# A macaron block on one core: z split straight out of PSUM, y evicted by halves, all jobs in a new order

## The chip, the core and the metric

The kernel runs on one core of a Trainium2 chip. Its time is the device time in microseconds (us) of one execution. TensorE (PE in the profile) multiplies, VectorE (DVE), ScalarE (ACT) and GpSimd (POOL) compute on tiles, SyncE (SP) starts most transfers. SBUF is the core's memory for operands, PSUM the one that TensorE writes to. Each engine works through its own queue of instructions in the order in which the program emits them, and waits on semaphores for the others.

## The reference

Four batches of 1024 tokens of width 128 in float32 go through three residual steps:

```python
x = L0_attn_x                                   # (4, 1024, 128)
x = x + 0.5 * ffn(layernorm(x))
x = x + mixer(layernorm(x))                     # x of this line is layernormed first; the mixer adds its own input too
x = x + 0.5 * ffn(layernorm(x))

def ffn(h):                                     # one routing decision for each batch of 1024 tokens
    logits = mean over the tokens of h @ gate_w # 8 experts
    top 2, their softmax weights normalised to sum 1
    out = sum of weight_e * (gelu(h @ w1[e] + b1[e]) @ w2[e] + b2[e])    # F = 512

def mixer(h):
    xn = clip(norm_scale * h / rms(h)); xc = silu(causal conv of 4 taps of xn)
    dt, v, gate = split(xc @ in_proj_w); dt = clip(softplus(dt + dt_bias))
    v = rope(v) * dt
    a decaying sum of v along the tokens, by chunks of 32, with a carry from chunk to chunk
    out = (heads mixed by a 16x16 matrix) * sigmoid(gate) @ out_proj_w;  return h + out
```

## The kernel before

The tokens of a batch lie in xt, [128 tokens, 8 tiles, 128 features], and stay in SBUF for the whole kernel. The two feed-forward steps are eight passes: pass q is batch q % 4, passes 0 to 3 are the first step and 4 to 7 the second. The mixer of batch b runs between pass b and pass b + 4, spread over the passes in between, so that its work on VectorE, ScalarE and GpSimd lies beside TensorE's feed-forward work.

**A pass.** VectorE takes the statistics of x (pass_stats), GpSimd makes 1/sqrt(var + eps) of them (pass_rstd: f_ve, then f_rstd), VectorE normalises into f_tok (pass_normalise), TensorE transposes that into aux_ps (pre_norm). ScalarE's turn_z copies aux_ps back into f_tok and sums over the tokens on the way (L570, into zsum, with an accumulator read), then rounds that copy to z_hi (L574), the part of z that the fast float32r matmul takes whole. VectorE's split_z subtracts z_hi from the copy in f_tok, which gives the rest z_lo (L1125). TensorE's pre_route (L953) multiplies zsum by the gate matrix, again into aux_ps; VectorE's route takes the two best experts of it (MAX, FIND_INDEX), and their weights are loaded and split into high and low parts likewise. The tile of the split first weights is w1_parts in the order of the instructions and w_parts in the trace.

**A slot.** Each pass has 8 slots (2 experts x 4 tiles of F), 64 in all. up(slot) is 6 matmuls of 128x512 into hid_ps: w_hi by z_hi, w_hi by z_lo, w_lo by z_hi, each for two halves of the tokens (L845). gelu(slot) on ScalarE makes hid of it (L639). down(slot) adds the slot's part to y in y_ps: in passes 0 to 4 with 8 matmuls for 8 token tiles (L873, in float32, y with tokens on the partitions); in passes 5 to 7 y is computed transposed, most slots by parts hid_hi and hid_lo in float32r (6 matmuls of 128x512, L898), the others whole. hid_ps has 2 buffers, hid 4, y_ps one. down is emitted a good slot after its up. The last three slots are computed apart (down_tail).

**The end of a pass.** In passes 0 to 4, update_x adds y_ps times coef to xt by halves (L1248), and waits for bias_added as well: token_bias on GpSimd computes the weighted b2 of the two experts (L486, L489) and adds it to xt with an accumulating DMA from GpSimd's queue (L494). The first down of the next pass waits until update_x has read y_ps, half by half. In passes 5 to 7 pass_out on ScalarE evicts y to yt with scale and bias (L670), in one piece in passes 5 and 6 and in two in pass 7; post on TensorE transposes yt into aux_ps (L965), and update_x adds that to xt. There the first down of the next pass waits for all of yt, once.

**aux_ps.** It is one PSUM tile of 128x1024, and all of TensorE's work beside up and down goes through it: norm, route, post, and the mixer's norm, dt, v, gate, heads and out. take_aux links them in the order in which they are emitted: whoever writes next waits until the last reader of the previous content is done, by halves where that reader works by halves. Before the change the reader of a norm is L570 (semaphore zt_ready).

**The order.** It is written out by hand, as numbers. A slot is 40 ticks; up(s) stands at tick 40 s on TensorE, gelu(s) at 40 (s + 1) on ScalarE, down(s) at 40 s + 98, or + 132 by parts. The table AT gives for each engine the tick of every other job. Each engine's program runs over the ticks and emits what stands at each; ticks are no times, they set an engine's order alone. Semaphores do the rest, so a job that is emitted early holds its whole engine until its input is there.

## Time and profile before

| | us |
|---|---|
| median of 3 runs | 260.31 (260.23 to 260.34) |
| profiled execution | 260.13 |
| its span in the trace | 258.3 |
| outside the span | 1.8 |
| TensorE busy in the span | 251.7 |

The span runs from the first to the last instruction of the profile. Sums against the trace are made against the 260.13 of the same execution, whose mean granted clock of TensorE was 0.997 of full. In the profile, busy time of a matmul is modelled at its end, and matmuls overlap a little, so an operation's row in a timeline may start a tenth or two before its piece in the chain of waits. A time in brackets behind a row is how long the engine sat idle before it, and for whom. A chain piece is a stretch of the sequence of work that ended last; where nothing waits, consecutive pieces touch.

### The profile page before, as it was taken

To read this page: it belongs to the slowest core of one execution; us is meant where nothing else is said; L and a number is where in the kernel's file an instruction comes from. 1 tells how busy PE (TensorE), PEld (TensorE's weight loads), DVE (VectorE), ACT (ScalarE), POOL (GpSimd) and SP (SyncE) were. 2 spreads that over 40 slices of the span, in tenths; PEclk is the share of its full clock that TensorE was granted. 3 is DMA by queue.
4 is the path that set the end of the run, shared out by engine and by line. 5 is a ranking of instruction groups with operands and counts; after the bars stand their busy time and mean duration, and the time that the engine had idled before them with its cause. 6 is when DMAs were issued, how large, how long until landed. Compare 5 with 4: busy or idle time off the path is not lost.

```text
span 258.3 us, 4609 instructions
## 1 busy us (share of the span) xinstructions
PE 251.7 (97%) x1540; PEld 218.6 (85%) x1540; DVE 211.1 (82%) x536; ACT 195.1 (76%) x236; POOL 82.9 (32%) x90
## 2 busy tenths in 40 slices
PE   7999999999999999999999999999999999999994
PEld 7979999998998979899979999878678687887894
DVE  4656587798589799999999999999999998675712
ACT  1255664866999877968848989999989957979650
POOL 5225306920019700995502957500306002000000
PEclk9999999999999999999999999999999999999998
DMA  6589749855100077430700700700007000570022
GB/s 194 176 255 338 121 81 362 177 221 206 63 0 0 13 94 242 47 38 9 260 0 0 81 4 0 247 0 0 0 4 246 0 0 3 155 229 24 0 84 82
DMA packets 21975, 26.18 MB, mean 101 GB/s; under 512 B 1280, under 2 KB 17152, under 8 KB 21952
## 3 DMA queue, kind: packets, MB, share of 16 engines
q1 hardware_dynamic: 15312, 22.39, 26.6%
q0 software_dynamic: 5280, 2.88, 9.3%
q10 hardware_dynamic: 1360, 0.62, 0.9%
q8 instruction: 12, 0.20, 0.3%
q14 instruction: 11, 0.09, 0.1%
HBM read 16.98 MB, written 6.29 MB: 90 GB/s over the span
## 4 chain that ended last, share of the span: by engine, by line
PE 91%; ACT 3%; issue 2%; DMA 1%; DVE 1%; POOL 0%; SPq 0%; DVEq 0%; ACTq 0%; POOLq 0%
PE hid_ps L845 32%; PE y_ps L873 28%; PE y_ps L898 10%; PE aux_ps L984 5%; PE aux_ps L940 4%; PE aux_ps L1016 3%; PE aux_ps L1005 3%; PE hid_ps L1023 2%; PE y_ps L917 1%; PE aux_ps L965 1%; ACT hid L639 1%; DMA m_tok<-wpack_dram 1%; ACT late L729 1%; PE y_ps L1028 1%; PE hid_ps L917 1%
## 5 line engine op out<-in xcount | busy, mean ns | idle before, releaser
L845 PE MATMUL hid_ps<-z_hi,w_parts 128*128 128x512 f32 x256 | 83.9, 410 | 0.4 <-ACT w_parts L592 0.4
L873 PEld LDWEIGHTS y_ps<-w_sb,hid 128*128 128x128 f32 x640 | 77.1, 192 | 4.3 <-DMA w_sb<-wpack_dram 0.8
L873 PE MATMUL y_ps<-w_sb,hid 128*128 128x128 f32 x640 | 78.1, 275 | 0.4 <-ACT hid L639 0.4
L639 ACT ACTIVATE hid<-hid_ps,w_sb 128x1024 f32<-128x1024 f32 x56 | 61.8, 1109 | 16.7 <-PE hid_ps L845 16.4
L845 PEld LDWEIGHTS hid_ps<-z_hi,w_parts 128*128 128x128 f32 x256 | 45.2, 189 | 9.5 <-issue 1.4
L845 PE MATMUL hid_ps<-z_lo,w_parts 128*128 128x512 f32 x128 | 40.1, 394 | 0.0
L1223 DVE TENSOR_TENSOR hid_lo<-hid,hid_hi 128x1024 fp32r<-128x1024 f32 x19 | 22.9, 1218 | 7.8 <-ACT hid_hi L646 7.8
L845 PEld LDWEIGHTS hid_ps<-z_lo,w_parts 128*128 128x128 f32 x128 | 24.0, 188 | 5.6
L646 ACT ACTIVATE hid_hi<-hid 128x1024 fp32r<-128x1024 f32 x19 | 19.6, 1054 | 1.3 <-PE y_ps L898 1.2
L486 POOL TENSOR_SCALAR bias_tok<-w_sb,coef 128x128 f32<-128x128 f32 x10 | 7.3, 734 | 39.1 <-DMA w_sb<-wpack_dram 25.2
L1110 DVE TENSOR_SCALAR f_tok<-xt,f_mv,f_rstd 128x128 f32<-128x128 f32 x64 | 17.7, 351 | 2.0 <-POOL f_rstd L464 1.9
L1089 DVE BATCH_NORM_STATS2 f_stat<-xt 128x6 f32<-128x128 f32 x64 | 13.1, 276 | 5.4 <-DMA xt<-x_dram 5.3
L530 POOL TENSOR_SCALAR small<-mix_tmp 128x32 f32<-128x32 f32 x4 | 4.3, 1080 | 40.7 <-DVE cumd L1337 40.7
L1294 DVE SCALAR_TENSOR_TENSOR xc<-xs,vec_sb,xc 128x1024 f32<-128x1024 f32 x12 | 15.3, 1276 | 1.8 <-ACT xc L692 1.7
L474 POOL TENSOR_SCALAR f_ve<-f_mv 128x8 f32<-128x8 f32 x7 | 2.4, 343 | 44.4 <-DVE f_mv L1092 44.3
L464 POOL TENSOR_TENSOR f_rstd<-f_ve,neg_half 128x8 f32<-128x8 f32 (+1 forms) x9 | 14.5, 1608 | 2.9 <-DVE f_ve L1096 2.3
L639 ACT ACTIVATE hid<-hid_ps,b_first 128x1024 f32<-128x1024 f32 x8 | 8.9, 1110 | 7.0 <-PE hid_ps L845 6.9
L684 ACT ACTIVATE xt<-xt,m_shift,m_gain 128x128 f32<-128x128 f32 x32 | 12.7, 483 | 0.0
L898 PE MATMUL y_ps<-hid_hi,w_hi 128*128 128x512 f32 x38 | 12.5, 410 | 0.0
L898 PE MATMUL y_ps<-hid_lo,w_hi 128*128 128x512 f32 x38 | 11.9, 394 | 0.0
L898 PE MATMUL y_ps<-hid_hi,w_lo 128*128 128x512 f32 x38 | 11.8, 393 | 0.0
L1125 DVE TENSOR_TENSOR z_lo<-f_tok,z_hi 128x1024 fp32r<-128x1024 f32 x7 | 8.6, 1233 | 3.3 <-ACT z_hi L574 3.1
(149 smaller groups left out, 465.4 us busy)
## 6 DMA issues: line engine op xcount, KB each, us to landing
w_parts<-w_split SPq DMA_DIRECT2D x12, 512.0 KB, 4.1
w_split<-mix_tmp SPq DMA_DIRECT2D x8, 512.0 KB, 4.9
w_sb<-wpack_dram SPq DMA_DIRECT2D x9, 322.5 KB, 4.0
xt<-bias_tok POOLq DMA_DIRECT2D x5, 512.0 KB, 6.5
late<-wpack_dram SPq DMA_DIRECT2D x2, 1024.0 KB, 7.1
w_sb<-wpack_dram SPq DMA_DIRECT2D x6, 258.5 KB, 4.3
xt<-x_dram SPq DMA_DIRECT2D x3, 512.0 KB, 8.4
out_dram<-xt SPq DMA_DIRECT2D x3, 512.0 KB, 3.2
```

The source lines that it names most:

```text
L464: nc.gpsimd.tensor_tensor(f_rstd[:, tiles], f_ve[:, tiles], neg_half[:, 0, tiles], ALU.pow).then_inc(done, 1)
L639: nc.scalar.activation(hid[:, slot % HBUF, :], hid_ps[:, slot % 2, :], ACT.Gelu, bias=bias).then_inc(hid_ready, 1)
L646: nc.scalar.activation(hid_hi[:, slot % 2, :], hid[:, slot % HBUF, :], ACT.Copy).then_inc(hid_hi_ready, 1)
L684: nc.scalar.activation(xt[:, b, t, :], xt[:, b, t, :], ACT.Identity, bias=m_shift[:, t:t + 1], scale=m_gain[:, t:t + 1]).then_inc(x_plus_h, 1)
L845: last = nc.tensor.matmul(hid_ps[:, slot % 2, cols], w, z[:, q % 2, cols], start=first, stop=end)
L873: last = nc.tensor.matmul(y_ps[:, cols], hid[:, slot % HBUF, cols], w_sb[:, q % 2, k, W2_AT + f * P:W2_AT + (f + 1) * P], start=t == 0 and ...
L898: last = nc.tensor.matmul(y_ps[:, cols], wt, src[:, cols], start=t == 0 and i == 0, stop=slot + 1 in (SLOTS * (q + 1), TAIL[0]) and end)
L984: last = nc.tensor.matmul(aux_ps[:, cols], wt[:, w, :], z[:, cols], start=first, stop=end)
L1089: V.bn_stats(f_stat[:, t, :], xt[:, b, t, :]).then_inc(f_stats_step, 1)
L1110: V.tensor_scalar(f_tok[:, t, :], xt[:, q % B, t, :], f_mv[:, t, 0:1], f_rstd[:, t:t + 1], ALU.subtract, ALU.mult).then_inc(f_norm_done, 1)
L1223: V.tensor_tensor(hid_lo[:, slot % 2, :], hid[:, slot % HBUF, :], hid_hi[:, slot % 2, :].bitcast(F32), ALU.subtract).then_inc(hid_lo_ready, 1)
L1294: V.scalar_tensor_tensor(xc[:, :], xs[:, k:k + N], conv_w[:, k:k + 1], xc[:, :], ALU.mult, ALU.add).then_inc(conv_step, 1)
```

## The change

Three things are changed.

**z.** turn_z is one ScalarE instruction in place of two: it rounds aux_ps to z_hi and sums on the way. split_z subtracts z_hi from aux_ps. f_tok is no longer written by ScalarE. So the last reader of a norm's aux_ps is z_lo (zlo_ready), for which the next writer of aux_ps, mostly route, waits; pass_normalise no longer waits for z_lo.

**y of passes 5 to 7.** pass_out always evicts two halves. In the last slot of such a pass, down runs all terms of the first half of the tokens and then those of the second, and a new semaphore y_half_up tells ScalarE of the first. The next pass's first down waits for yt by halves, and post too.

**The order.** Every number of AT is set anew; the slots' own offsets stay.

```diff
-        "f_norm": {1: 189, 2: 389, 3: 809, 4: 1149, 5: 1509, 6: 1829, 7: 2166},
+        "f_norm": {1: 189, 2: 309, 3: 789, 4: 1169, 5: 1509, 6: 1806, 7: 2166},
...
-        "f_bias": {0: 144, 1: 375, 2: 877, 3: 974, 4: 1363},
+        "f_bias": {0: 289, 1: 513, 2: 718, 3: 1205, 4: 1432},
...
                 act.wait_ge(f_turned, q + 1)
                 act.wait_ge(logits_up, q)
-                f_feat = f_tok[:, :, :].rearrange("p t d -> p (t d)")
-                nc.scalar.activation(f_feat, aux_ps[:, :], ACT.Copy, accum_out=zsum[:, 0:1]).then_inc(zt_ready, 1)
-                act.wait_ge(zt_ready, q)
                 if q >= 2:
                     act.wait_ge(hid_up, SLOTS * (q - 1))
-                nc.scalar.activation(z_hi[:, q % 2, :], f_feat, ACT.Copy).then_inc(zhi_ready, 1)
+                nc.scalar.activation(z_hi[:, q % 2, :], aux_ps[:, :], ACT.Copy,
+                                     accum_out=zsum[:, 0:1]).then_inc(zhi_ready, 1)
...
-                for i, cols in enumerate(parts_of(q, N)):
-                    act.wait_ge(hid_used, (SLOTS * (q + 1) if q < PASSES - 1 else TAIL[0]) + i)
+                for half in range(2):
+                    cols = slice(half * HALF, (half + 1) * HALF)
+                    if half:
+                        act.wait_ge(hid_used, last_turned(q) + 1)
+                    else:
+                        act.wait_ge(y_half_up, turned_passes(q + 1))
                     nc.scalar.activation(yt[:, cols], y_ps[:, cols], ACT.Identity,
                                          bias=bias2[:, q % 2, :], scale=coef[:, q % 2, 0:1]).then_inc(yt_ready, 1)
...
-                if t == 0 and q and not in_tokens(q - 1):
-                    pe.wait_ge(yt_ready, turned_passes(q))
...
+                steps = [(i, half) for i in range(len(terms)) for half in range(2)]
+                if slot == last_turned(q):
+                    steps = [(i, half) for half in range(2) for i in range(len(terms))]
...
+                    elif t == 0 and i == 0 and q:
+                        pe.wait_ge(yt_ready, 2 * turned_passes(q) - 1 + half)
...
+                    if slot == last_turned(q) and end and half == 0:
+                        last.then_inc(y_half_up, 1)
...
             def pre_norm(q):
-                free = take_aux(zt_ready, q, q)
+                free = take_aux(zlo_ready, q + 2, q + 2)
...
-                pe.wait_ge(zt_ready, q)
+                pe.wait_ge(zhi_ready, q + 1)
                 free = take_aux(index_ready, q + 1, q + 1)
...
                     dve.wait_ge(f_turned, q)
-                    if q >= 2:
-                        dve.wait_ge(zlo_ready, q + 1)
...
-                V.tensor_tensor(z_lo[:, q % 2, :], f_tok[:, :, :].rearrange("p t d -> p (t d)"),
+                V.tensor_tensor(z_lo[:, q % 2, :], aux_ps[:, :],
                                 z_hi[:, q % 2, :].bitcast(F32), ALU.subtract).then_inc(zlo_ready, 1)
```

Three places show how the new numbers move the instructions. For the same operation the line number of after is a few higher than that of before.

**First, GpSimd in pass 0.** f_ve and f_rstd are the statistics of pass 1 and of pass 2; bias_tok and the DMA are token_bias of pass 0. Before:

```order
L474 TENSOR_SCALAR f_ve<-f_mv 128x8
L464 TENSOR_TENSOR f_rstd<-f_ve,neg_half 128x8
L486 TENSOR_SCALAR bias_tok<-w_sb,coef 128x128 x2
L489 TENSOR_TENSOR bias_tok<-bias_tok 128x128
L494 DMA xt<-bias_tok 128x8x128
L474 TENSOR_SCALAR f_ve<-f_mv 128x8
L464 TENSOR_TENSOR f_rstd<-f_ve,neg_half 128x8
```

After:

```order
L475 TENSOR_SCALAR f_ve<-f_mv 128x8
L465 TENSOR_TENSOR f_rstd<-f_ve,neg_half 128x8
L475 TENSOR_SCALAR f_ve<-f_mv 128x8
L465 TENSOR_TENSOR f_rstd<-f_ve,neg_half 128x8
L487 TENSOR_SCALAR bias_tok<-w_sb,coef 128x128 x2
L490 TENSOR_TENSOR bias_tok<-bias_tok 128x128
L495 DMA xt<-bias_tok 128x8x128
```

The bias and its DMA have moved behind the statistics of pass 2. Those wait for VectorE's BN_AGGR of pass 2, on VectorE at the same place. Here f_tok is the normalise of pass 1 (L1110, L1112) and z_lo the rest of pass 1's z; before:

```order
L1110 TENSOR_SCALAR f_tok<-xt,f_mv,f_rstd 128x128 x8
L1089 BN_STATS f_stat<-xt 128x6 x8
L1092 BN_AGGR f_mv<-f_stat 128x2 x8
L1217 TENSOR_SCALAR w_sb<-w_sb,ratio 128x512
L1125 TENSOR_TENSOR z_lo<-f_tok,z_hi 128x1024
L1418 TENSOR_SCALAR proj_sb<-proj_sb 128x512
```

After:

```order
L1112 TENSOR_SCALAR f_tok<-xt,f_mv,f_rstd 128x128 x8
L1148 ISA
L1148 TENSOR_TENSOR w1_parts<-late,w1_parts 128x256
L1152 TENSOR_TENSOR w1_parts<-m_tok,w1_parts 128x256
L1127 TENSOR_TENSOR z_lo<-aux_ps,z_hi 128x1024
L1219 TENSOR_SCALAR w_sb<-w_sb,ratio 128x512
L1093 BN_STATS f_stat<-xt 128x6 x8
L1096 BN_AGGR f_mv<-f_stat 128x2 x8
L1174 MAX top_v<-aux_ps 128x8
```

z_lo and the scaling of the second weights (w_sb) stood behind the statistics of pass 2 and now stand ahead of them.

**Second, TensorE at slot 42.** aux_ps<-proj_sb,late is m_out of batch 2, the six matmuls from silu are m_dt of batch 3, and hid_ps is an up. Before:

```order
L845 MATMUL hid_ps<-z_hi,w1_parts 128x512 x2
L1016 MATMUL aux_ps<-proj_sb,late 128x128 x8
L845 MATMUL hid_ps<-z_hi,w1_parts 128x512 x2
L845 MATMUL hid_ps<-z_lo,w1_parts 128x512 x2
L845 MATMUL hid_ps<-z_hi,w1_parts 128x512 x2
L984 MATMUL aux_ps<-silu_hi,proj_hi 128x512
L984 MATMUL aux_ps<-silu_hi,proj_lo 128x512
L984 MATMUL aux_ps<-silu_lo,proj_hi 128x512
L984 MATMUL aux_ps<-silu_hi,proj_hi 128x512
```

After:

```order
L848 MATMUL hid_ps<-z_hi,w1_parts 128x512 x2
L1020 MATMUL aux_ps<-proj_sb,late 128x128 x8
L988 MATMUL aux_ps<-silu_hi,proj_hi 128x512
L988 MATMUL aux_ps<-silu_hi,proj_lo 128x512
L988 MATMUL aux_ps<-silu_lo,proj_hi 128x512
L988 MATMUL aux_ps<-silu_hi,proj_hi 128x512
L988 MATMUL aux_ps<-silu_hi,proj_lo 128x512
L988 MATMUL aux_ps<-silu_lo,proj_hi 128x512
L848 MATMUL hid_ps<-z_hi,w1_parts 128x512 x2
```

The up that stood between m_out and m_dt has moved behind m_dt.

**Third, TensorE at the end of pass 6.** aux_ps<-gate_sb,zsum is route 7, aux_ps<-ident,yt is post 5, y_ps a down by parts. Before:

```order
L898 MATMUL y_ps<-hid_hi,w2_lo 128x512 x2
L898 MATMUL y_ps<-hid_lo,w2_hi 128x512 x2
L953 MATMUL aux_ps<-gate_sb,zsum 128x8
L845 MATMUL hid_ps<-z_hi,w1_parts 128x512 x2
L845 MATMUL hid_ps<-z_lo,w1_parts 128x512 x2
L845 MATMUL hid_ps<-z_hi,w1_parts 128x512 x2
L965 MATMUL aux_ps<-ident,yt 128x128 x8
```

After:

```order
L906 MATMUL y_ps<-hid_hi,w2_lo 128x512 x2
L906 MATMUL y_ps<-hid_lo,w2_hi 128x512 x2
L848 MATMUL hid_ps<-z_hi,w1_parts 128x512 x2
L848 MATMUL hid_ps<-z_lo,w1_parts 128x512 x2
L848 MATMUL hid_ps<-z_hi,w1_parts 128x512 x2
L959 MATMUL aux_ps<-gate_sb,zsum 128x8
L969 MATMUL aux_ps<-ident,yt 128x128 x8
```

The up that stood between route 7 and post 5 now stands ahead of both.

## Rows read from the trace of the kernel before

**Rows 1.** The profile's page, busy time of each engine, share of the span, instructions.

```profile
PE 251.7 (97%) x1540; PEld 218.6 (85%) x1540; DVE 211.1 (82%) x536; ACT 195.1 (76%) x236; POOL 82.9 (32%) x90
```

**Rows 2.** Windows: busy us of PE, PEld, DVE, ACT, POOL; PE clock, DMA share, GB/s.

```profile
180.00:200.00 20.00, 19.45 (x86) 14.69 (x85) 19.41 (x41) 18.84 (x21) 6.82 (x5) 1.00 0.23 81
...
240.00:258.00 18.00, 14.77 (x93) 12.93 (x92) 6.43 (x10) 6.98 (x7) 0.00 (x0) 0.97 0.21 60
```

**Rows 3.** Timelines of TensorE and ScalarE, first down; then the chain: start, us, what.

```profile
14.29 0.42 ACT L609 ACTIVATE w_parts<-m_tok 128x256 fp32r<-128x256 f32 x1 [1.00 <-DMA m_tok<-wpack_dram]
...
15.85 2.02 PE L873 MATMUL y_ps<-w_sb,hid 128*128 128x128 f32 x16 [0.39 <-ACT hid L639]
...
24.22 0.87 PE aux_ps L940 x8
...
43.42 1.78 PE y_ps L873 x16
```

**Rows 4.** Chain, one TensorE timeline row at 186.99, and the waits for L570.

```profile
83.05 2.04 PE y_ps L873 x16
...
219.83 0.26 PE aux_ps L953 x2
...
233.58 1.61 PE y_ps L898 x6
...
236.57 1.39 PE y_ps L898 x6
...
186.99 1.96 PE L898 MATMUL y_ps<-hid,w_sb 128*128 128x512 f32 x4 [0.55 <-ACT hid L639]
...
PEld aux_ps L953 <- ACT f_tok L570: 0.6, 2, 0.3
```

**Rows 5.** By line: duration ns min/median/max, first and last start; last, one timeline row.

```profile
L574 ACT ACTIVATE z_hi<-f_tok x7: 1057/1058/1060, 28.7 to 219.6; 128x1024 fp32r<-128x1024 f32 x7
...
L1125 DVE TENSOR_TENSOR z_lo<-f_tok,z_hi x7: 1217/1226/1270, 29.8 to 224.9; 128x1024 fp32r<-128x1024 f32 x7
...
L670 ACT ACTIVATE yt<-y_ps,bias,coef x4: 772/991/1208, 204.9 to 247.7; 128x1024 f32<-128x1024 f32 x2, 128x512 f32<-128x512 f32 x2
...
150.33 1.22 DVE L1362 TENSOR_TENSOR late<-aux_ps,rope_sb 128x1024 f32<-128x1024 f32 x1
```

**Rows 6.** Timeline of GpSimd (POOL), 16 to 32 us.

```profile
19.51 1.20 POOL L486 TENSOR_SCALAR bias_tok<-w_sb,coef 128x128 f32<-128x128 f32 x2
...
21.57 1.67 POOL L494 DMA_DIRECT2D xt<-bias_tok  x1 [0.31 <-POOL bias_tok L489]
...
26.37 0.36 POOL L474 TENSOR_SCALAR f_ve<-f_mv 128x8 f32<-128x8 f32 x1 [3.14 <-DVE f_mv L1092]
...
26.82 1.67 POOL L464 TENSOR_TENSOR f_rstd<-f_ve,neg_half 128x8 f32<-128x8 f32 x1
```

**Rows 7.** Timeline of VectorE (DVE), 20 to 44 us.

```profile
24.08 1.65 DVE L1089 BATCH_NORM_STATS2 f_stat<-xt 128x6 f32<-128x128 f32 x8 [1.97 <-DMA xt<-x_dram]
...
40.37 1.65 DVE L1248 SCALAR_TENSOR_TENSOR xt<-y_ps,coef,xt 128x512 f32<-128x512 f32 x2 [1.39 <-PE y_ps L873]
```

**Rows 8.** Landing of the bias DMA (L494), and SP's DMA issues in its timeline.

```profile
DMA to landing us min/median/max: 6.4/6.5/9.5
...
34.50 1.49 SPq L412 DMA_DIRECT2D w_sb<-wpack_dram  x2
...
36.10 20.16 SPq L420 DMA_DIRECT2D w_split<-mix_tmp  x8
```

**Rows 9.** Timeline of GpSimd, the carry of batch 2.

```profile
157.98 2.24 POOL L531 TENSOR_SCALAR ncd<-cumd 128x32 f32<-128x32 f32 x1
```

**Rows 10.** Timeline of VectorE ahead of the mixer's add of batch 2.

```profile
172.03 1.28 DVE L1403 SCALAR_TENSOR_TENSOR late<-late,aux_ps 128x512 f32<-128x512 f32 x2
...
173.23 1.22 DVE L1307 TENSOR_TENSOR silu_lo<-silu,silu_hi 128x1024 fp32r<-128x1024 f32 x1
```

**Rows 11.** Timeline of VectorE, route of pass 7.

```profile
220.41 0.16 DVE L1179 FIND_INDEX8 top_i<-top_v,aux_ps 128x8 uint32<-128x8 f32 x1
```

More of the change, by code:

```diff
@@ L90 @@
[L90 to L95 removed]
+        "c_split_rest": {0: 113, 1: 168},
@@ new lines @@
+        "m_cos": {0: 767, 1: 1131, 2: 1476, 3: 1800},
+        "m_decay": {0: 779, 1: 1080, 2: 1437, 3: 1817},
+        "m_u": {0: 814, 1: 1210, 2: 1514, 3: 1912},
+        "m_carry": {0: 829, 1: 1193, 2: 1563, 3: 1910},
+        "m_dstep": {0: 830, 1: 1170, 2: 1533, 3: 1925},
+        "m_u2": {0: 860, 1: 1225, 2: 1565, 3: 1948},
+        "m_scan": {0: 893, 1: 1237, 2: 1609, 3: 1970},
+        "m_scan2": {0: 914, 1: 1263, 2: 1639, 3: 1995},
+        "m_gated": {0: 982, 1: 1356, 2: 1683, 3: 2062},
@@ L117 @@
+        "y_out": {5: 1992, 6: 2310, 7: 2500},
     },
     "pool": {
[L119 to L123 removed]
+        "f_rstd": {1: 40, 2: 170, 3: 543, 4: 887, 5: 1451, 6: 1648, 7: 1949},
+        "f_bias": {0: 289, 1: 513, 2: 718, 3: 1205, 4: 1432},
@@ L129 @@
+        "y_store": {4: 2259, 5: 2447, 6: 2477},
     },
@@ L889, in down @@
                     terms = [(w2, hid[:, slot % HBUF, :], None)]
-                for i, (wt, src, ready) in enumerate(terms):
-                    if ready:
-                        pe.wait_ge(ready, split_slots(slot))
-                    for half in range(2):
-                        cols = slice(half * HALF, (half + 1) * HALF)
-                        end = i == len(terms) - 1
-                        if t == 0 and i == 0 and q and in_tokens(q - 1):
-                            pe.wait_ge(x_updated, 2 * q - 1 + half)
-                        last = nc.tensor.matmul(y_ps[:, cols], wt, src[:, cols], start=t == 0 and i == 0,
-                                                stop=slot + 1 in (SLOTS * (q + 1), TAIL[0]) and end)
-                        if slot == TAIL[0] - 1 and end and half == 0:
-                            last.then_inc(hid_used, 1)
+                steps = [(i, half) for i in range(len(terms)) for half in range(2)]
+                if slot == last_turned(q):
+                    steps = [(i, half) for half in range(2) for i in range(len(terms))]
+                for i, half in steps:
+                    wt, src, ready = terms[i]
+                    if ready and half == 0:
+                        pe.wait_ge(ready, split_slots(slot))
+                    cols = slice(half * HALF, (half + 1) * HALF)
+                    end = i == len(terms) - 1
+                    if t == 0 and i == 0 and q and in_tokens(q - 1):
+                        pe.wait_ge(x_updated, 2 * q - 1 + half)
+                    elif t == 0 and i == 0 and q:
+                        pe.wait_ge(yt_ready, 2 * turned_passes(q) - 1 + half)
+                    last = nc.tensor.matmul(y_ps[:, cols], wt, src[:, cols], start=t == 0 and i == 0,
+                                            stop=slot == last_turned(q) and end)
+                    if slot == last_turned(q) and end and half == 0:
+                        last.then_inc(y_half_up, 1)
                 last.then_inc(hid_used, 1)
             def down_tail():
-                pe.wait_ge(yt_ready, turned_passes(PASSES) + 1)
+                pe.wait_ge(yt_ready, 2 * turned_passes(PASSES))
                 pe.wait_ge(w2_scaled, scaled_passes(PASSES))
```

132 lines of the change are left out of this document (60 added, 72 removed), and 6 rows, old and new, of the table AT.

## The prediction

> **What bounds the kernel now.** Read the busy times first: TensorE works 251.7 us of the span of 258.3, VectorE 211.1, ScalarE 195.1 [rows 1]. Then the table by stretches, for where TensorE's 6.6 idle us lie: 0.55 in 180 to 200 and 3.23 after 240 [rows 2]; most of the other 2.8 lies before the first down. The ends are code that the change leaves alone: the warm-up, the first routing and the load that the first up waits for, and the last VectorE updates and stores. So what the change can win is what TensorE waits or works slowly between its first down and its last post. There the profile has four kinds of places, all small; I look at each with TensorE's timeline, where a down that has waited for ScalarE shows either idle time in brackets or a duration above its fellows':
> - the first down, idle 0.39 before it and 2.02 long where a down that hasn't waited takes 1.78 [rows 3]: 0.63. Ahead of gelu 0 on ScalarE stands L609, which waited 1.00 for its load [rows 3].
> - down 19, 2.04 instead of 1.78 [rows 3, 4]: 0.26, gelu 19 behind a table load.
> - down 43, 0.55 idle, and I give 0.2 to the slow restart: 0.75 [rows 4].
> - the routing matmuls of passes 6 and 7, whose weight load waits 0.3 each time for L570, of which about 0.14 reaches the matmuls: 0.28; and down 56, 1.61 instead of 1.39, behind the eviction of y: 0.22 [rows 4].
>
> Together 2.14 us. That is the ceiling of a gain: 260.13 - 2.1 = 258.0. In the stretch with the long wait VectorE is busy 19.41 of 20 us and ScalarE 18.84 [rows 2], so a freed engine helps only where the other one isn't late as well.
>
> **The z part.** It removes L574 seven times, 7 x 1.06 = 7.4 us of ScalarE [rows 5]; the accumulator read stays. It lies beside TensorE and is worth what the waits above are worth, no more. z_lo stays one VectorE instruction, now with PSUM as one source. L1125 from SBUF takes 1.23, and L1362, also a tensor_tensor of 128x1024 but out of PSUM, 1.22 [rows 5]: cost nothing. What does change is that aux_ps is held until z_lo has read it: route now waits for z_lo, one VectorE instruction later than before, and the next pass's normalise waits no longer. Where route stands behind an up or a down (all passes), 1.2 us fit in that cover; without it route would cost TensorE up to 1.2 each.
>
> **The y part.** Passes 5 and 6 evict in two pieces of 0.77 us where one piece takes up to 1.21 [rows 5]: up to 0.33 more of ScalarE twice, but the first half can start while TensorE still does the other. I take down 56's 0.22 back, and nothing else.
>
> **The order: the places that the old cover has left.** All terms are on TensorE, against "due", the old start less the 0.63 of the first down.
>
> *The bias of pass 0.* This is the large one. GpSimd (POOL) made bias_tok at 19.51 and started its DMA at 21.57; only then it took the statistics of pass 2, f_ve and f_rstd, 26.37 to 28.49 [rows 6]. Now both come first. f_rstd 2 needs VectorE's f_stats 2, and that now stands behind z_lo 1 and the scaling of w2. norm 1 leaves TensorE at 24.22 + 0.87 - 0.63 = 24.5 [rows 3] (its place is unchanged), z_hi 1 is one instruction with its accumulator read, 1.15 to 1.2: 25.7; z_lo 1.23: 26.9; the scaling of 512 columns, 0.4 by estimate: 27.3; from the start of the statistics to that of f_ve as before (24.08 to 26.37 [rows 6, 7], 2.3): 29.6; f_ve and f_rstd 2.1: 31.7; bias from 19.51 to 21.57, 2.1: the DMA starts at 33.8 instead of 21.57. It takes 6.4 to 9.5 us to land [rows 8]: 6.4 or 6.5 mostly, 9.5 the first time, beside large loads. In the old trace SP's queue issues w_sb twice at 34.50 and w_split from 36.10 on [rows 8], and this comes at about the same time now, so the bias won't be alone: I take 9.5 as the low end of "shared", 43.3, and as the high end an even split, where 6.4 less 1.67 for issuing [rows 6] counts twice: 33.8 + 1.67 + 9.46 = 44.9. The Trainium skill ("DMA: Bandwidth & Descriptors", Queues, rings and completion order) says that a DMA engine takes turns between its queues packet by packet, which speaks for the even split; by a free road it would land at 40.2.
> Who waits: update 0 (L1248), 1.65 for two halves [rows 7], waits for the DMA; down 8 writes y_ps and waits for the first half, 0.8 and a hop after the landing: 0.9. Down 8 started at 43.42 and is due at 42.8 [rows 3]. So a landing by 41.9 costs nothing, 43.3 costs 1.4, 44.9 costs 3.0. I take 43.8 (nearer to the row than to the split, since not all loads are there at once): **1.9**. Behind update 0 on VectorE stand the splits for SP, m_stats 0 and z_lo 2, which have slack of a slot or two.
>
> *Five small ones.*
> - gelu 38: m_carry 2 now starts on GpSimd about 158.75. In the old trace one of its steps, on 32 columns, took 2.24 us [rows 9]. With a chain of 3.0 us in all I get ScalarE's decay and its table loads out so that down 38 is 0.3 late; each us more is one more, so a step like the old one would make it about 1.3. I take 0.3.
> - m_out 2 and m_dt 3 now stand directly behind each other on TensorE, with no up between. m_dt 3 writes aux_ps and must wait for m_add's first half, which follows gated and silu_lo on VectorE. These ran from 172.03 to 174.4 [rows 10]; a half of the add is one more piece like a half of gated, 0.64, so 175.1. m_out ends at 174.5: 0.6. Bounds 0 (if m_add gets in ahead) and 1.3.
> - down 40 needs w2_lo, now behind f_stats 6: 0.15.
> - gelu 47 now stands behind m_decay 3 and its table loads: 0.4, set between down 19's 0.26 and down 43's 0.55, which waited for ScalarE in the same way; 0 to 1.3.
> - post 5 now stands directly behind route 7, which it follows in aux_ps; it waits until MAX and FIND_INDEX have read the logits, 219.83 to 220.57 in the old trace [rows 4, 11]: 0.6 with the hop.
>
> Sum 2.05. That eats the 2.14 won.
>
> **The sum.** 260.13 - 2.14 + 2.05 + 1.9 = 261.9. The profiled execution lies 0.18 under the median (260.31), so the median of after is **262.1**.
>
> **Rivals.**
> *A, the bias lands late, as above.* Landing 43.3 to 44.9, small ones 1.5 to 2.3: 261.1 to 263.4 in the median.
> *B, the bias is in time.* For: a lone one took 6.4, and 33.8 + 6.4 = 40.2 is before 41.9. Against: the loads at 34.50. Small ones as reckoned: 260.31 - 0.1 = 260.2, no change.
> *C, not slower, and faster: the bias is in time and the small waits stay out.* Mechanism: 7.4 us less on ScalarE let gelu run ahead, so that carry, silu_lo and the table loads are reached earlier than I reckon from old times; it decides from about 1 us of lead on either engine at 160 to 180. 260.31 - 2.14 + 0.3 = 258.5. For: VectorE's 19.41 of 20 shows that it, not data, paces that stretch, and it loses the wait behind L574. Against: VectorE itself has not a microsecond less to do.
> *D, the bias late and the small waits out:* 258.5 + 1.9 = 260.4, no change.
> *E, more slips.* Everything behind update 0 arrives late and a carry of 4.0 us costs 1.3: 263.0 to 264.
> *F, the change doesn't do what it says* (z_hi and its sum in one instruction takes as long as two, as would show in a ScalarE row of 2 us at z_hi): then there is no lead, and the 2.14 are not won: 263 to 264; I count it with E.
>
> **How the numbers follow.** A 0.48, B 0.14, C 0.17, D 0.13, E with F 0.08. The prediction is A's, 262.1. The range leaves out C and E's upper part: 259.8 to 263.2. A measurement of this kernel can tell about 0.2%, 0.52 us, from no change. Faster than 259.8: C and a bit of B and D, 0.20. Within: most of B and D, 0.21. Slower than 260.8: A, E and a bit of D, 0.59.
>
> **What would show it.** In TensorE's waits a new one of 1 to 3 us at the down line, at about 43, for VectorE's update, which itself waits for the DMA xt<-bias_tok; if there is none, A's main step is wrong. A wait at post at about 221 for top_i, and one at the projection at about 174.5 for xt. No ScalarE wait for m_tok ahead of gelu 0, down 19 at 1.78, and no idle time at 187. The forecast is wrong if the bias's DMA starts clearly before 33 us, or if the sum of the small waits is under 1 us.

## The result

The changed kernel takes 262.07 us in the median of 6 runs (261.72 to 264.76), the kernel before, measured beside it, 260.22 (259.27 to 260.34). The ratio is 1.009, with a 95% interval of 1.0051 to 1.0128: slower by about 1%. Measured once more beside the kernel before, it took 262.77 against 259.51, ratio 1.0109 (1.0088 to 1.0129). The ratios of this document leave out two executions, of 317 and 424 us, whose granted clock was low.

The page of after, the row that answers to [rows 1]: TensorE has 254.3 us of work in a span of 263.0, ScalarE 188.6 instead of 195.1.

```profile
PE 254.3 (97%) x1540; PEld 220.4 (84%) x1540; DVE 211.8 (81%) x536; ACT 188.6 (72%) x231; POOL 76.1 (29%) x90
```

This profiled execution took 264.76 us, 2.7 more than the median of its kernel, so I take the figures below from a second profiled execution of the same kernel (label after_again, 262.88 us, span 261.1) wherever the two differ, and come back to the 2.7 at the end. TensorE's waits in that second one (engine, what it waited to do, for whom: us in total, times, longest):

```profile
PE y_ps L876 <- ACT hid L638: 1.8, 1, 1.8
...
PE aux_ps L988 <- ACT mix_tmp L718: 0.6, 1, 0.6
...
PE aux_ps L969 <- DVE top_i L1181: 0.5, 1, 0.5
...
PE aux_ps L988 <- DVE xt L1414: 0.3, 1, 0.3
```

The first is at down 8, at 44 us. Who was late there, in the timelines of the first profile of after: GpSimd's DMA of the bias and its landing, SP's load of w_sb, then VectorE's update 0, ScalarE's gelu 8 and TensorE's down 8. They answer to [rows 3, 6 to 8].

```profile
29.80 0.24 POOL L475 TENSOR_SCALAR f_ve<-f_mv 128x8 f32<-128x8 f32 x1 [11.45 <-DVE f_mv L1096]
...
33.86 1.67 POOL L495 DMA_DIRECT2D xt<-bias_tok  x1 [0.32 <-POOL bias_tok L490]
...
35.07 0.36 SPq L421 DMA_DIRECT2D w_split<-mix_tmp  x1
...
36.24 2.15 SPq L413 DMA_DIRECT2D w_sb<-wpack_dram  x2
...
43.65 1.41 DVE L1250 SCALAR_TENSOR_TENSOR xt<-y_ps,coef,xt 128x512 f32<-128x512 f32 x2 [4.44 <-DMA xt<-bias_tok]
...
43.74 2.12 ACT L638 ACTIVATE hid<-hid_ps,w_sb 128x1024 f32<-128x1024 f32 x2 [4.77 <-DMA w_sb<-wpack_dram]
...
44.95 3.34 PE L876 MATMUL y_ps<-w_sb,hid 128*128 128x128 f32 x16 [1.82 <-ACT hid L638]
```

The bias's DMA starts at 33.86 where it started at 21.57, and lands 9.8 us later, at 43.6. But the row of ScalarE says more: gelu 8 had stood for 4.77 us on w_sb of pass 1, the tile with the second weights and with the bias that the gelu adds. Its first load was issued at 36.24 and landed 7.4 us later, within 0.1 us of the bias. gelu 8 takes 1.1 us, update 0 only 0.75 for its first half, so the gelu is what down 8 waited for in the end.

Where the rest of the time went shows best in the times of the 64 ups on TensorE. The table takes the start of each up's third matmul, its first with z_lo, and gives each kernel's difference from the kernel before (us, plus is later). Slots are chosen where both orders have done the same TensorE work. What a difference grows by from one column to the next is called a step; the kernels that aren't named yet are those of the experiments.

```
slot                     1      9     10     20     31     37     41     48     53     58     63
before, start        14.39  42.33  45.50  81.96 129.21 156.28 172.30 198.78 216.48 232.46 247.45
after (first)        +0.05  -0.27  +3.40  +3.43  +3.54  +4.32  +4.67  +4.23  +4.57  +5.23  +4.98
after_again          -0.27  -0.59  +1.46  +1.44  +1.56  +2.34  +2.42  +2.30  +2.68  +3.34  +3.09
bias_first           -1.01  -1.31  -1.33  -1.35  -1.22  -0.42  -0.39  -0.54  -0.20  +0.46  +0.21
load_first           -0.70  -1.03  +0.10  +0.10  +0.22  +1.01  +1.04  +0.89  +1.22  +1.88  +1.62
stats_first          -0.35  -0.68  +0.16  +0.15  +0.27  +1.05  +1.06  +0.93  +1.27  +1.94  +1.68
repaired             -1.01  -1.34  -1.35  -1.36  -1.22  -0.57  +0.65  +0.18  +0.17  +1.16  +0.91
old_code_new_order   -0.71  -0.57  +1.77  +2.13  +3.08  +4.06  +4.52  +5.35  +5.70  +6.89  +6.92
new_code_old_order   +0.06  +0.78  +0.77  +2.08  +8.50  +8.49 +10.85 +12.76 +12.75 +14.01 +13.75
y_only               -0.80  -0.75  -0.76  -0.78  -0.79  -0.78  -0.78  -0.76  -0.77  -0.77  -1.01
y_one_number         -0.76  -0.86  -0.87  -0.90  -0.85  -0.86  -0.86  -0.84  -0.83  -0.84  -1.10
```

The first column isn't the change: even y_only, whose program is the same up to 200 us, starts 0.8 earlier than before did, and bias_first 1.0. Behind slot 10 the steps of after_again, bias_first, load_first and stats_first repeat to within 0.1. In after_again they are: -0.32 from slot 1 to 9, +2.05 at slot 10, +0.1 up to slot 31, +0.8 from 31 to 37, nearly nothing from 37 to 48, +0.38 from 48 to 53, +0.66 from 53 to 58, -0.25 from 58 to 63. Together +3.36 after the start. The first profile of after has the same steps there except +0.35 instead of +0.08 from 37 to 41: its up 40 began only when the weights of pass 5 (w_parts) had landed, at 171.5.

### The profile page after: what moved, and what is told of

It is laid out like the page before. It is cut to its first block, busy times and chain, and to the rows that moved or that the text cites. A ratio compares the mean times of both kernels' runs of the same rounds, so it can differ in the third digit from the quotient of the medians.

```text
span 263.0 us, 4592 instructions
## 1 busy us (share of the span) xinstructions
PE 254.3 (97%) x1540; PEld 220.4 (84%) x1540; DVE 211.8 (81%) x536; ACT 188.6 (72%) x231; POOL 76.1 (29%) x90
## 3 DMA queue, kind: packets, MB, share of 16 engines
HBM read 16.98 MB, written 6.29 MB: 88 GB/s over the span
## 4 chain that ended last, share of the span: by engine, by line
PE 78%; DVE 9%; DMA 4%; issue 3%; ACT 2%; POOL 1%; SPq 1%; DVEq 0%; ACTq 0%; POOLq 0%
PE hid_ps L848 28%; PE y_ps L876 20%; PE y_ps L906 11%; PE aux_ps L988 5%; DMA w_sb<-wpack_dram 3%; PE aux_ps L946 3%; PE aux_ps L1009 2%; PE hid_ps L1027 2%; PE aux_ps L1020 2%; DMA w_parts<-w_split 2%; DVE f_tok L1112 1%; PE y_ps L923 1%; PE aux_ps L969 1%; DVE mix_tmp L1324 1%; POOL f_rstd L465 1%
## 5 line engine op out<-in xcount | busy, mean ns | idle before, releaser
L876 PEld LDWEIGHTS y_ps<-w_sb,hid 128*128 128x128 f32 x640 | 78.2, 194 | 6.0 <-issue 3.1
L876 PE MATMUL y_ps<-w_sb,hid 128*128 128x128 f32 x640 | 79.6, 278 | 1.9 <-ACT hid L638 1.8
L475 POOL TENSOR_SCALAR f_ve<-f_mv 128x8 f32<-128x8 f32 x7 | 4.7, 671 | 68.0 <-DVE f_mv L1096 68.0
L1112 DVE TENSOR_SCALAR f_tok<-xt,f_mv,f_rstd 128x128 f32<-128x128 f32 x64 | 17.6, 348 | 4.1 <-POOL f_rstd L465 3.9
L1127 DVE TENSOR_TENSOR z_lo<-aux_ps,z_hi 128x1024 fp32r<-128x1024 f32 x7 | 8.5, 1213 | 5.9 <-ACT z_hi L572 5.9
L1250 DVE SCALAR_TENSOR_TENSOR xt<-y_ps,coef,xt 128x512 f32<-128x512 f32 x10 | 7.2, 745 | 7.2 <-DMA xt<-bias_tok 5.2
```

Of the source, the lines that this page charges most:

```text
L876: last = nc.tensor.matmul(y_ps[:, cols], hid[:, slot % HBUF, cols], w_sb[:, q % 2, k, W2_AT + f * P:W2_AT + (f + 1) * P], start=t == 0 and ...
L1112: V.tensor_scalar(f_tok[:, t, :], xt[:, q % B, t, :], f_mv[:, t, 0:1], f_rstd[:, t:t + 1], ALU.subtract, ALU.mult).then_inc(f_norm_done, 1)
```

## The experiments

**The same kernel again.** No edit.

> The changed kernel once more, nothing edited. The first trace of it had two waits that ended within half a microsecond of each other at about 44 us: ScalarE's gelu 8 for the weights of pass 1 (w_sb landed 7.4 us after its issue), and VectorE's update 0 for the bias of pass 0 (landed 9.8 us after its issue); down 8 began at 44.95 where 42.8 was due, and TensorE's clock then fell for some us, 2.7 us over the median of the other executions. Theory 1 (the loads share the DMA engines, so where they end varies by 1 to 2 us): 262.0 again, and this trace shows down 8 at 43.3 to 45, the clock mostly at its upper level. Theory 2 (the first trace is typical and the later stretch is better than it looks): down 8 at 44.9 again.

262.77 (262.06 to 262.88). The step at slot 10 is 2.05, against 3.67 in the first profile, with the same idle time before down 8: 1.83 here and 1.82 there.

```profile
44.64 2.02 PE L876 MATMUL y_ps<-w_sb,hid 128*128 128x128 f32 x16 [1.83 <-ACT hid L638]
```

So theory 2 was right as to the wait, which is the same in both to 0.01 us, and theory 1 as to the clock, which fell only in the first (below). The median is 0.8 above the 262.0 that theory 1 had.

**The bias first.**

```diff
-        "f_bias": {0: 289, 1: 513, 2: 718, 3: 1205, 4: 1432},
+        "f_bias": {0: 144, 1: 513, 2: 718, 3: 1205, 4: 1432},
```

> One number of the changed kernel: token_bias of pass 0 stands at tick 144 on GpSimd again, ahead of the rstd of pass 2. Its DMA starts at about 19 instead of 33.9 and is down by 30. Theory 1 (the bias is what down 8 waits for, or what keeps the w_sb loads long): down 8 at 42.8 to 43.2, time 260.2 to 260.7. Theory 2 (the w_sb loads, issued at 36.2 behind the first w_split, are late on their own): they still land at 41 or later, gelu 8 waits, time 261.0 to 262.

260.06 (259.73 to 260.71), ratio to before 1.002 (1.0007 to 1.0034), 2.7 us under after_again beside it. GpSimd's DMA and ScalarE's gelu 8:

```profile
19.60 1.64 POOL L495 DMA_DIRECT2D xt<-bias_tok  x1 [0.32 <-POOL bias_tok L490]
...
38.96 1.11 ACT L638 ACTIVATE hid<-hid_ps,w_sb 128x1024 f32<-128x1024 f32 x1 [1.04 <-PE hid_ps L848]
```

Down 8 waits for nothing. The loads of w_sb still stand behind the first w_split on SP:

```profile
34.79 1.75 SPq L413 DMA_DIRECT2D w_sb<-wpack_dram  x2
```

That is 1.1 us earlier than in after_again (35.92), and 0.7 of that is the earlier start of this execution. But the first of them lands 2.9 us after its issue where it took 7.4 there, and gelu 8 waits for TensorE and not for it. So w_sb was late because of the bias's DMA beside it, and theory 1 holds. Of the 2.7 us between the medians the step at slot 10 is 2.05. The other steps are the same; the starts of the two profiled executions differ by 0.7.

**The loads first.** On SP, the first w_split behind the load of pass 1's weights.

```diff
-        "c_pre_out": {0: 321, 1: 359, 2: 420, 3: 428, 4: 478, 5: 490, 6: 524, 7: 554},
+        "c_pre_out": {0: 328, 1: 359, 2: 420, 3: 428, 4: 478, 5: 490, 6: 524, 7: 554},
```

> One number of the changed kernel: on SP the load of pass 1's weights (w_sb twice) stands ahead of the first w_split, so that it is issued when route 1 is done, at about 30.5 instead of 36.2. Theory 1 (the bias's DMA is what down 8 waits for): gelu 8 does not wait, but the bias starts at 33.9 as before and lands at 40.5 to 43; time 260.5 to 261.8. Theory 2 (the w_sb loads alone made the wait): down 8 at 42.8, 260.2.

261.56 (260.97 to 262.02), 1.2 us under after_again. Now w_sb is in time (issued from 30.06 on, landed at 32.9 and 35.9) and only the bias is late: its DMA starts at 33.10, has two w_split beside it (34.32 and 34.91) and lands 9.3 us later; the update begins at 42.38, and TensorE waits for it.

```profile
33.10 1.67 POOL L495 DMA_DIRECT2D xt<-bias_tok  x1 [0.32 <-POOL bias_tok L490]
...
42.38 1.41 DVE L1250 SCALAR_TENSOR_TENSOR xt<-y_ps,coef,xt 128x512 f32<-128x512 f32 x2 [3.93 <-DMA xt<-bias_tok]
...
PE y_ps L876 <- DVE xt L1250: 0.9, 1, 0.9
```

The step at slot 10 is 1.13. So of the 2.05 the late bias made 1.13 without w_sb beside it, and w_sb 0.9 more.

**Both.** The two edits together.

> Both numbers: the bias at tick 144 on GpSimd, the loads ahead of the first w_split on SP. All theories: no wait at 43, down 8 at 42.8. What is left against the kernel before is then the rest of the new order: if the small waits that I reckoned (2.05) cancel the removed ones, 260.1 to 260.5; if there is a new one of 0.8 at the projection of v at 150, as the trace of after shows, 260.6 to 261.0.

260.25 (259.71 to 260.94), ratio 1.0027 (1.0013 to 1.0042), no step at slot 10 (-0.02), the rest of the slots as in bias_first. The time lies in the first of the two ranges that were expected, 260.1 to 260.5, but those were reckoned from a kernel before at 260.3, and the one beside it took 259.51. By the ratio it is 0.7 us slower, and the slots say +1.08 between slot 1 and 63. So the second reading holds, with the new wait of 0.8: the small waits of the new order are worth more than what it saves.

**The bias late, in the kernel before.**

```diff
-        "f_bias": {0: 144, 1: 375, 2: 877, 3: 974, 4: 1363},
+        "f_bias": {0: 289, 1: 375, 2: 877, 3: 974, 4: 1363},
```

> The kernel before with one number changed: token_bias of pass 0 at tick 289 on GpSimd, behind the rstd of pass 2. Theory 1 (what hurts in the changed kernel is the whole chain: z_lo 1 and the scaling of w2 ahead of f_stats 2 on VectorE, f_rstd 2, and only then the bias): here f_stats 2 is as early as ever, the bias's DMA starts at 30.6 and lands by 37 to 40.5, before update 0 wants it at 40.4; no wait, time as before, within 0.2%. Theory 2 (the order on GpSimd alone does it, since the bias shares the DMA engines with the loads in any case): landing 41 to 43, 0.5 to 2 us slower.

259.66 against 259.27, ratio 1.0014 (1.0004 to 1.0023). Its slots stand at -0.89 to -0.84 against the kernel before from the first to the last, so in its profile nothing costs anything; the 0.4 us between the medians, within the 0.2% that was expected, isn't seen there. The DMA starts at 30.74 and lands 6.8 us later (the five bias DMAs of this kernel land 6.5 to 6.8 us after their issue); the loads come 4.0 us after it.

```profile
30.74 1.64 POOL L494 DMA_DIRECT2D xt<-bias_tok  x1 [0.31 <-POOL bias_tok L489]
...
DMA to landing us min/median/max: 6.5/6.7/6.8
...
34.74 2.12 SPq L412 DMA_DIRECT2D w_sb<-wpack_dram  x2
```

**The statistics first, in the changed kernel.** On VectorE, ahead of z_lo 1.

```diff
-        "f_stats": {1: 86, 2: 236, 3: 361, 4: 1017, 5: 1410, 6: 1721, 7: 2093},
+        "f_stats": {1: 86, 2: 216, 3: 361, 4: 1017, 5: 1410, 6: 1721, 7: 2093},
```

> One number of the changed kernel: on VectorE the statistics of pass 2 stand at tick 216, ahead of z_lo 1 and the scaling of w2, as in before; GpSimd's order stays (rstd of pass 2 ahead of the bias). Theory 1 (the length of the chain makes the bias late): the statistics start at 24, rstd 2 is done at 28.2, the bias's DMA starts at 30.3 and lands at 37 to 40.5: no wait at down 8, 260.0 to 260.5. Theory 2 (the bias behind rstd 2 is enough to be late in this order, since w_split and w_sb also start earlier and meet it): landing 41 to 43, 260.7 to 262.

260.56 (259.94 to 262.06), ratio 1.0046 (1.0023 to 1.0069), between the ranges of the two theories. Theory 1 said no wait, and there is one of 0.6 at down 8, for the update; the step at slot 10 is 0.84. The DMA starts at 30.12, 0.6 earlier than in the run above, and lands 12.3 us later:

```profile
30.12 1.67 POOL L495 DMA_DIRECT2D xt<-bias_tok  x1 [0.32 <-POOL bias_tok L490]
...
31.34 0.36 SPq L421 DMA_DIRECT2D w_split<-mix_tmp  x1
...
32.50 2.12 SPq L413 DMA_DIRECT2D w_sb<-wpack_dram  x2
...
42.44 1.41 DVE L1250 SCALAR_TENSOR_TENSOR xt<-y_ps,coef,xt 128x512 f32<-128x512 f32 x2 [6.96 <-DMA xt<-bias_tok]
```

The rstd of pass 2 is not only ahead of the bias on GpSimd. By the order of the program it also lets the normalise of pass 2 go, then the split of the first expert, then SP's w_split and the loads behind that. Here the chain is 3.4 us faster than in after_again, and the loads have moved with it: w_split and w_sb are 1.2 and 2.4 us behind the bias in both. So it is both: the chain's length, which makes the difference between 2.05 and 0.84, and that what releases the bias releases the loads too. In the kernel before with the bias late the loads wait for route 1 and come 4 us after the bias; that is why it is harmless there.

**The old code in the new order, and the new code in the old order.** The first is the code of before with the table of after. The second is the reverse, with z_lo ahead on VectorE where route and the mixer now wait for it:

```diff
-        "f_split_z": {1: 262, 2: 526, 3: 990, 4: 1217, 5: 1571, 6: 1895, 7: 2261},
+        "f_split_z": {1: 262, 2: 500, 3: 870, 4: 1201, 5: 1567, 6: 1889, 7: 2201},
```

> The code of before with the table of after: only the order of the jobs is new; z is copied to f_tok and rounded from there again, y of passes 5 and 6 evicted in one piece. Theory 1 (the time goes to the order, mostly to pass 0's bias): z_lo 1 comes 1.06 later than in after, so the bias starts at 34.9 and down 8 is later by up to 1: slower than before by 2.5 to 4.5 us. Theory 2 (the new code itself costs something in the later stretch): not slower than after.

> The new code for z and y with the table of before, in which z_lo of passes 2 to 7 had to move ahead on VectorE by 3 to 120 ticks, since route now waits for it. Theory 1 (the new code is worth its small waits, those of routes 6 and 7 and of down 56, some 0.5 us, and ScalarE's 7.4 us hide): 0.2 to 1.0 us faster than before. Theory 2 (holding aux_ps until z_lo is done makes the routing or the mixer wait on TensorE): same or slower, with TensorE waits at the routing line for z_lo.

267.68 (ratio 1.032, 1.0307 to 1.0334) and 273.86 (ratio 1.0537, 1.0498 to 1.0576). Both are far slower than the changed kernel. The waits of TensorE, first in the old code with the new order, then in the new code with the old order:

```profile
PE y_ps L873 <- ACT hid L639: 2.8, 3, 2.1
...
PE aux_ps L965 <- DVE top_i L1179: 1.2, 1, 1.2
...
PE aux_ps L959 <- DVE z_lo L1127: 6.9, 5, 2.2
...
PE aux_ps L946 <- DVE z_lo L1127: 4.3, 2, 3.2
...
90.37 1.97 PE L946 MATMUL aux_ps<-ident,m_tok 128*128 128x128 f32 x8 [3.21 <-DVE z_lo L1127]
```

In the second, TensorE waits 6.9 us at five routes (L959) and 4.3 at two norms (L946) for z_lo. One of them, 3.21 at 90, is the mixer's norm right behind the norm of pass 3: z_lo stands behind other VectorE work, and aux_ps is held all that time. Theory 2 holds there. The loss hangs on where I put z_lo in that table; a better place wasn't tried, so this kernel doesn't say what the new code would be worth in an order near the old one. In the first, my range of 2.5 to 4.5 was too low: 8.4 against the before beside it. It loses 2.34 at slot 10, like after, then 1.4 us more than after_again from slot 10 to 37 and 2.1 more from there to slot 63, at downs that wait for their gelu and at post 5 (1.2 where after has 0.5). So the new code, with 7.4 us less on ScalarE, is worth 4 us by the slots and 5 by the medians in the new order, and the new order without it is far slower than the old one.

**Four numbers repaired.** bias_first, and the three places where its slots lose:

```diff
-        "m_v": {0: 709, 1: 1089, 2: 1429, 3: 1726},
+        "m_v": {0: 709, 1: 1089, 2: 1449, 3: 1726},
-        "y_turn_y": {5: 2208, 6: 2446, 7: 2600},
+        "y_turn_y": {5: 2245, 6: 2446, 7: 2600},
-        "m_decay": {0: 820, 1: 1186, 2: 1546, 3: 1912},
+        "m_decay": {0: 820, 1: 1186, 2: 1546, 3: 1933},
-        "f_bias": {0: 289, 1: 513, 2: 718, 3: 1205, 4: 1432},
+        "f_bias": {0: 144, 1: 513, 2: 718, 3: 1205, 4: 1432},
```

> The changed kernel with four numbers set otherwise: token_bias of pass 0 at 144 on GpSimd (as in bias_first), m_v 2 on TensorE behind the next up (1449), post 5 on TensorE behind the next up (2245), and m_decay 3 on ScalarE behind gelu 47 (1933). Each takes away one wait that the slots' times of bias_first show against before: 0.8 at 146, 0.54 to 0.66 at 222, 0.14 to 0.35 at 201. If these are real terms of the sum: 260.06 - 1.6 = 258.5, about 1 us faster than before. If another wait takes their place (gelu 35 behind the swap's table load, the eviction of y of pass 6 behind a later post): 259.3 to 260.1.

260.24 (259.8 to 260.96), ratio 1.0033 (1.0019 to 1.0047): no better than bias_first, and within the range of the second reading. One of the three came: with m_decay 3 behind gelu 47 the step of 0.35 at slot 49 is gone. The other two came back as other waits (this profiled execution took 260.71):

```profile
PE aux_ps L946 <- DVE late L1364: 0.4, 1, 0.4
...
PE hid_ps L848 <- DMA w_parts<-w_split: 0.8, 1, 0.8
...
PE y_ps L906 <- DVE hid_lo L1225: 0.7, 1, 0.7
```

With m_v 2 one up later TensorE is 0.8 ahead, and then the mixer's norm waits 0.4 for VectorE's rotation (L1364). That rotation hasn't moved. Here it is in bias_first and in this run:

```profile
150.42 1.19 DVE L1364 TENSOR_TENSOR late<-aux_ps,rope_sb 128x1024 f32<-128x1024 f32 x1
...
150.40 1.20 DVE L1364 TENSOR_TENSOR late<-aux_ps,rope_sb 128x1024 f32<-128x1024 f32 x1
```

VectorE worked without a pause from 146.8 on in both, so it, and not the wait that I took away, set the time there: of the 0.8 us 0.15 are left at slot 37. Post 5 one up later is the same: the down that now stands ahead of it starts earlier and waits 0.7 for hid_lo, which stands behind route 7 on VectorE as in bias_first (222.12 here, 221.74 there, with everything in this run 0.38 later at that point); the step from slot 53 to 58 is 0.98 with the repair and 0.67 without. The wait of 0.8 at the up at 167.5 is another matter. w_parts of pass 5 was issued at the same time in both, 162.4, and took 5.1 us to land here and 3.5 there. The traces don't show why; in before, after, after_again, load_first, bias_load_first and stats_first it took 3.4 to 4.3.

**y alone.** The kernel before with its table and the y part only.

> The kernel before, with its table, and only the y part of the change: y of passes 5 to 7 evicted by halves, the last down of such a pass half by half, the waits for yt by halves. z as before. Theory 1 (worth down 56's wait): down 56 takes 1.39 instead of 1.61, the slots from 59 on are 0.2 to 0.3 earlier, time 0.2 to 0.3 us less than before, within 0.2%. Theory 2 (the second eviction's fixed part delays hid_hi): same or slower.

259.23 against 259.55, ratio 0.9987 (0.9973 to 1.0002): within what can be told. The slots show it nevertheless, a step of -0.25 at slot 59 and nothing else. Down 56, which took 1.61 [rows 4], in the chain of y_only:

```profile
232.78 1.40 PE y_ps L908 x6
```

**y and two numbers, y and one number.** On ScalarE, the split of the rest of the first weights (L609) behind gelu 0, and in the first of the two kernels the swap of batch 3 behind gelu 43 as well.

```diff
-        "c_split_rest": {0: 19, 1: 60},
+        "c_split_rest": {0: 60, 1: 60},
...
-        "m_swap": {0: 733, 1: 1060, 2: 1413, 3: 1750},
+        "m_swap": {0: 733, 1: 1060, 2: 1413, 3: 1761},
```

> y_only and two numbers on ScalarE: the rest of the first weights (L608) behind gelu 0 (tick 60 instead of 19), and the swap of batch 3 behind gelu 43 (1761 instead of 1750). The first is in the changed kernel too and was worth 0.32 there. The second should take away the 0.55 of idle time before down 43. If both come and nothing takes their place: y_only less 0.9 us, so about 1.1 us faster than before. If the swap, 1.3 us later, holds aux_ps for norm 6 or VectorE's rotation: y_only less 0.3 or slower.

> y_only (the kernel before with y of passes 5 to 7 by halves) and one number: the rest of the first weights on ScalarE behind gelu 0 (tick 60 instead of 19). The traces of y_two_numbers and y_only give the two terms as 0.33 at slot 2 and 0.25 at slot 59, and the other number of y_two_numbers as a loss of 0.8. So 0.6 us less than the kernel before, 0.2%: at the edge of what can be told, but with the lower time of the two. If the terms are no terms (the start of the program differs from execution to execution by up to 1 us in any kernel): the ratio's interval includes 1.

With both: 259.84 against 259.55, ratio 1.001 (0.9994 to 1.0027). The idle 0.55 before down 43 is gone, but the step at slot 45 is +0.64: norm 6 now waits for VectorE's normalise. The swap is what has pushed that back: VectorE's rotation ahead of it now stands idle for ScalarE, which it didn't in y_only.

```profile
185.67 1.22 DVE L1368 TENSOR_TENSOR late<-aux_ps,rope_sb 128x1024 f32<-128x1024 f32 x1 [1.17 <-ACT late L734]
...
187.29 2.03 PE L948 MATMUL aux_ps<-ident,f_tok 128*128 128x128 f32 x8 [0.29 <-DVE f_tok L1116]
```

With c_split_rest alone: 258.98 against 259.82, ratio 0.9972 (0.9957 to 0.9987). The slots say 0.33 at slot 2, of which 0.2 are lost again at slot 3 in this execution and not in the one of y_two_numbers, and 0.25 at slot 59. It is the fastest kernel of the study, faster than the kernel before by 0.28%, a little more than the 0.2% that can be told. Down 0 there, to be held against [rows 3]:

```profile
14.76 2.02 PE L878 MATMUL y_ps<-w_sb,hid 128*128 128x128 f32 x16
```

## Why the prediction was right, and where it was not

The forecast was 262.1, the range 259.8 to 263.2, slower as the likeliest. The measured median is 262.07, so the prediction was right in the time and in its main step. That the two agree so closely is luck: the small waits were mis-sized by more than a microsecond, as the terms show. All steps below are those of after_again.

- **The bias of pass 0, 1.9.** Right in place, cause and nearly in size. The DMA was forecast to start at 33.8 (33.86), to land at 43.8 (43.6), and the step is 2.05. The chain that I summed on VectorE and GpSimd ends within 0.1 us in the first profile and 0.3 in the second (33.53). Two things were missing. The last one to arrive was not the update but gelu 8, by half a us. I had SP's loads at "about the same time" as before and they were 1.7 later (36.24), since the new order puts the first w_split ahead of them, and that hangs on the same rstd. And the loads suffer from the bias as the bias does from them: w_sb took 7.4 us to land beside it and 2.9 without it, and of the 2.05 load_first leaves 1.13.
- **The first down, -0.63.** Half of it: -0.32. The idle 0.39 is gone but for 0.07, and down 0 still takes 2.02. This term was mis-sized, and with it the due time of down 8, by 0.3.
- **Down 19, -0.26.** Not won. Its place gets 0.1 worse by slot 22; another down (at 88.4 in after_again) takes 2.02.
- **Down 43, -0.75, m_out 2 with m_dt 3, +0.6, and down 40, +0.15.** Together nothing forecast, and -0.12 from slot 41 to 48. No idle time stands before down 40. The wait for xt is 0.3 idle and 0.24 in the out matmuls ahead.
- **gelu 38, +0.3.** Didn't come; slot 37 to 41 is +0.08, and +0.03 in bias_first.
- **gelu 47, +0.4.** 0.36.
- **Post 5, +0.6.** 0.66, of which 0.54 idle. It answers to [rows 11]:

```profile
224.71 1.09 PE L969 MATMUL aux_ps<-ident,yt 128*128 128x128 f32 x8 [0.54 <-DVE top_i L1181]
```

- **Down 56, -0.22.** -0.25.
- **The routes of passes 6 and 7, -0.28.** No step of that size between slots can be told from the others; left open.
- **Not foreseen: m_v 2, +0.8.** m_dt 2 moved on TensorE from tick 1349 to 1409, behind up 34 (the program has up(s) at tick 40 (s + 1), not at 40 s as told above), and on ScalarE behind gelu 34, so that its table load and its read of aux_ps come when m_v 2, 20 ticks behind, wants aux_ps. ScalarE's gelu 34, table load and read, and TensorE's m_v 2 in after_again:

```profile
144.92 1.12 ACT L638 ACTIVATE hid<-hid_ps,w_sb 128x1024 f32<-128x1024 f32 x1 [2.90 <-PE hid_ps L848]
...
146.05 1.28 ACT L712 ACT_TABLE_LOAD   x1
...
147.35 1.12 ACT L718 ACTIVATE mix_tmp<-aux_ps,vec_sb 128x1024 f32<-128x1024 f32 x1
...
148.61 0.47 PE L988 MATMUL aux_ps<-silu_hi,proj_hi 128*128 128x512 f32 x1 [0.56 <-ACT mix_tmp L718]
```

The step is 0.8, of which 0.56 is idle time. This is the largest miss among the small ones: I had looked for places where the up between two jobs went away, and here a down still stands between.

So the removed waits and the small new ones, which I had as -2.14 + 2.05 = -0.1, are in truth +1.3 (3.36 less 2.05). The whole is +3.4 after the start, not +1.8. The second measurement agrees (+3.3 at the medians); the first gave +1.85, with five of the six runs of before between 260.1 and 260.4, while beside the second they spread from 258.96 to 260.26. The start of the program, below, differs by as much from one execution to the next; that this is what parts the two measurements isn't shown. The mechanism of the main term was right, the terms of the small waits were mis-sized by 1.4 in sum. A sum with their true sizes would have given 260.31 + 1.31 + 2.05 = 263.7, above the range.

The rivals: bias_first shows that B's or C's premise (the bias in time) gives 260.06 against 259.51, +0.2%, so even then the small waits would have come, and C falls, and D with it. E's late carry didn't come (gelu 38), but its range, 263 to 264, is where the sum with the true sizes lies. F falls: the new z_hi takes 1.02 and 0.20 for the sum, and z_lo from PSUM 1.22, not more than from SBUF [rows 5]. The 0.45 us that the table in the Trainium skill ("VectorE: DVE Perf Modes", The TRN2 errata — SBUF-src ops pay a fixed extra latency per instruction) would give for the PSUM sources didn't appear.

```profile
L572 ACT ACTIVATE z_hi<-aux_ps x7: 1009/1018/1027, 24.9 to 223.2; 128x1024 fp32r<-128x1024 f32 x7
...
L572 ACT ACTIVATION_READ_ACCUMULATOR z_hi<-aux_ps x7: 193/202/210, 25.8 to 224.1; 128x1 f32 x7
...
L1127 DVE TENSOR_TENSOR z_lo<-aux_ps,z_hi x7: 1190/1216/1225, 26.0 to 224.3; 128x1024 fp32r<-128x1024 f32 x7
```

On the DMA the two readings of a landing, alone or shared, were both right: 6.8 us with the loads 4.0 us behind it (bias_late_only), 9.8 and 10.0 with w_split 1.2 and w_sb 2.4 us behind it (after, after_again), and 12.3 with the same two at the same distances (stats_first). Why the last is 2.3 to 2.5 longer than the others the traces don't show; it stays open. Nor is it only those loads: the bias DMA that starts at 19.60 in bias_first, with another load beside it (rope_sb, landed at 29.6), took 12.3 as well, where before's at 21.57 took 9.5. That transfers of two queues stretch each other fits the rule of turns that the forecast cited from the Trainium skill ("DMA: Bandwidth & Descriptors", Queues, rings and completion order), but 12.3 is above the 11.1 of an even split (1.67 + 9.46), so it isn't a full account.

## What to carry to other kernels

When a job that ends in a transfer is moved behind a wait, add up the whole chain to its new start, and ask what else the same chain releases: transfers that are let go by the same event meet each other, and each lands later (7.4 us instead of 2.9 for w_sb, 9.8 instead of 6.8 for the bias). A change that frees one engine and holds a shared buffer longer is worth what the order of the other engines makes of it; here the new order without the new code lost 8 us, the new code in the old order with only z_lo moved 14, both together 3. And a wait on the busiest engine is worth taking away only as far as the next engine isn't due at the same time: of three repairs one stayed, and the other two met VectorE, whose instructions had not moved at all.
